# A decoder layer on one core: the last tiles of cross attention reordered, and four running sums instead of six in the shared expert

## What is computed

```python
x = x + attn(layernorm(x), Wqkv, bqkv, Wo, bo)
x = x + xattn(layernorm(x), ctx, mask, Wq, ..., residual_scale)
x = x + ffn(layernorm(x), gate, Wg, Wu, Wd, Sg, Su, Sd)
# ffn:
scores = softmax(x @ gate.T)                       # 64 experts
topk_w, topk_i = top_k(scores within the best 3 of 8 groups, 6)
pos = rank of the token among those that chose the expert
out = (silu(buf @ Wg.T) * (buf @ Wu.T)) @ Wd.T     # per expert, 192 slots
y = sum(out[slot] * topk_w, axis=1)
shared = silu(x @ Sg.T) * (x @ Su.T) @ Sd.T        # 704 inner features
return y + shared
```

## Time and profile before

| | |
|---|---|
| runs | 1564.96, 1571.54, 1579.25 us (median 1571.54) |
| profiled execution | 1564.96 us, span 1563.2 us |
| mean granted TensorE clock | 0.979 |
| TensorE busy | 1481.2 us (95%) |
| VectorE busy | 1135.9 us (73%) |
| ScalarE busy | 957.2 us (61%) |
| GpSimd busy | 713.1 us (46%) |
| steps 12 to 15 of cross attention | 540.15 to 607.67 us |
| cross attention after its loop | 607.67 to 654.25 us |
| routed experts | from 656.6 us to about 1377 us |
| end of the feed-forward | about 1377 to 1563.2 us |

### The profile page before, as it was taken

The page is one execution under the profiler, slowest core; times in us unless marked ns, Lnnn a source line. Parts: engine busy times, 40 slices in busy tenths (PEclk is TensorE's granted clock), DMA queues, the critical chain, the costliest instruction groups (busy, mean ns, idle before and its releaser), DMA issues.

```text
span 1563.2 us, 30303 instructions
## 1 busy us (share of the span) xinstructions
PE 1481.2 (95%) x10344; PEld 1224.2 (78%) x10344; DVE 1135.9 (73%) x2032; ACT 957.2 (61%) x1890; POOL 713.1 (46%) x885
## 2 busy tenths in 40 slices
PE   6999998999999988689999999999999999999988
PEld 4788886778888766478888888888888888866766
DVE  6677666646888789558777777777777877767766
ACT  4566566644566665558777877777777777741110
POOL 2122225333232143246556565665656555447763
PEclk9999999999999999889999999999999999999998
DMA  6012212332121221299877787777877778367664
GB/s 209 1 62 82 61 49 69 102 98 69 62 80 50 76 88 45 99 365 335 273 264 266 261 294 268 265 262 269 295 264 264 261 275 287 130 205 242 188 189 148
DMA packets 116629, 280.25 MB, mean 179 GB/s; under 512 B 17984, under 2 KB 23104, under 8 KB 116544
## 3 DMA queue, kind: packets, MB, share of 16 engines
q1 hardware_dynamic: 98800, 228.25, 42.9%
q0 software_dynamic: 15360, 50.34, 10.1%
q10 hardware_dynamic: 2384, 0.53, 0.2%
HBM read 235.69 MB, written 43.38 MB: 179 GB/s over the span
## 4 chain that ended last, share of the span: by engine, by line
PE 51%; DVE 2%; issue 1%; SPq 1%; DMA 1%; ACT 0%; POOL 0%; DVEq 0%; POOLq 0%
PE e_gu L2575 18%; PE e_gu L2577 8%; PE e_dn_rest L2603 5%; PE e_dn_main L41 3%; PE e_tr L49 3%; PE e_dn_main L43 3%; PE e_dn_main L42 3%; PE h_dn L41 1%; PE h_dn L42 1%; PE h_dn L43 1%; DMA e_raw_d<-in_L_ffn_Wd_dram 1%; SPq L2283 1%; PE h_gt L43 1%; PE h_gt L41 1%; PE h_gt L42 1%
## 5 line engine op out<-in xcount | busy, mean ns | idle before, releaser
L2338 POOL TENSOR_TENSOR e_hid<-e_h_raw,e_hid 128x128 fp32r<-128x128 f32 (+1 forms) x192 | 166.2, 866 | 222.6 <-ACT e_hid L2403 222.5
L2575 PE MATMUL e_gu<-e_xT_hi_lo,e_wg 128*128 128x384 f32 (+1 forms) x768 | 232.2, 358 | 0.8 <-issue 0.6
L2575 PE MATMUL e_gu<-e_xT_hi_lo,e_wu 128*128 128x384 f32 (+1 forms) x768 | 230.6, 356 | 0.0
L2577 PE MATMUL e_gu<-e_xT_hi_lo,e_wu 128*128 128x192 f32 (+1 forms) x768 | 193.4, 252 | 0.0
L2577 PE MATMUL e_gu<-e_xT_hi_lo,e_wg 128*128 128x192 f32 (+1 forms) x768 | 193.3, 252 | 0.0
L2346 POOL TENSOR_TENSOR e_wd<-e_raw_d,e_wd 96x512 fp32r<-96x512 f32 x64 | 131.8, 2059 | 35.9 <-ACT e_wd L2388 35.9
L2575 PEld LDWEIGHTS e_gu<-e_xT_hi_lo,e_wg 128*128 128x128 f32 (+1 forms) x768 | 138.4, 180 | 6.5 <-issue 1.8
L2481 DVE TENSOR_TENSOR e_total<-e_gu,e_low 128x384 f32<-128x384 f32 (+1 forms) x192 | 105.5, 550 | 51.8 <-issue 41.3
L2398 ACT ACTIVATE e_low<-e_gu 128x384 f32<-128x384 f32 (+1 forms) x192 | 93.4, 486 | 80.7 <-PE e_gu L2577 73.6
L2577 PEld LDWEIGHTS e_gu<-e_xT_hi_lo,e_wg 128*128 128x128 f32 (+1 forms) x768 | 140.1, 182 | 1.4
L2575 PEld LDWEIGHTS e_gu<-e_xT_hi_lo,e_wu 128*128 128x128 f32 (+1 forms) x768 | 137.9, 180 | 3.8
(11 more groups left out here) (419 smaller groups left out, 3957.6 us busy)
## 6 DMA issues: line engine op xcount, KB each, us to landing
e_raw_g<-in_L_ffn_Wg_dram SPq DMA_DIRECT2D x64, 704.0 KB
e_raw_u<-in_L_ffn_Wu_dram SPq DMA_DIRECT2D x64, 704.0 KB
e_raw_d<-in_L_ffn_Wd_dram SPq DMA_DIRECT2D x64, 512.0 KB, 6.4
y_dram<-e_y_main SPq DMA_DIRECT2D x64, 256.0 KB
e_raw_d<-in_L_ffn_Wd_dram SPq DMA_DIRECT2D x64, 192.0 KB, 7.5
y_dram<-e_y_rest SPq DMA_DIRECT2D x64, 128.0 KB
s_xr<-in_x_dram SPq DMA_DIRECT2D x16, 256.0 KB, 4.1
x_dram<-s_x SPq DMA_DIRECT2D x16, 256.0 KB, 2.4
```

What stands on the lines that cost most here:

```text
L2338: pool.tensor_tensor(hid[b][1][0:n, c, :], h_raw[g.odd][b][0:n, c, 0:P], hid[b][0][0:n, c, :].bitcast(F32), ALU.subtract).then_inc(s_hl, 1)
L2575: pe.matmul(bank[0:n, 0:2 * CAP], w[b][0][:, k, m:m + n], xT[:, :, k, toks], start=k == 0, stop=False)
L2577: ins = pe.matmul(bank[0:n, 0:CAP], w[b][1][:, k, m:m + n], xT[:, 0, k, toks], start=False, stop=k == KC - 1)
```

## The change

It has two parts. In `cross_phase`, for steps t >= 12 (`LAST`): TensorE's `turn_final(t-2)` moves behind `project_out(t-1)`, VectorE's `final_lo(t-2)` behind `output(t-1)`, and VectorE's `row_sums(t)` ahead of `choose_experts`. In steps 14 and 15 the second early unit moves behind `project_out`, on TensorE, and behind the table entries, on ScalarE. After the loop, `widen`, `project_out` and several units move ahead, so that the units fill other places between the steps of the routing, and ScalarE copies one more gate (`COPIED` = 4) and makes the entries of the last full group before units 8 to 10. In `shared_programs` the sums have four buffers instead of six, so the residual of tile n+4 is loaded when `finish(n)` is done, and VectorE's `routed` halves go to other places: one tile fewer is summed ahead of a turn and two to three halves more are done between the chunks of turns 1 and 2.

```diff
-AHEAD_SUMS = 6
-COPIED = 3
+COPIED = 4
...
+        LAST = BATCH - XQ
...   # ScalarE, in the loop: behind the table entries instead of ahead
+                for i in EARLY_UNITS.get(t, ())[1:2]:
+                    shared_out(i)
...   # ScalarE, after the loop
             rinv_out(BATCH - 1)
+            attn_hi(BATCH - 1)
             shared_out(4)
-            attn_hi(BATCH - 1)
             final_norm(BATCH - 2)
             final_hi(BATCH - 2)
             table_entries(NG - 3, 0)
+            shared_out(5)
+            table_entries(NG - 3, 1)
             route_exp(BATCH - 2)
             final_norm(BATCH - 1)
-            shared_out(5)
+            shared_out(6)
             final_hi(BATCH - 1)
-            table_entries(NG - 3, 1)
             route_exp(BATCH - 1)
             for c in range(COPIED):
                 shared_gate(c)
-            shared_out(6)
             shared_out(7)
-            table_entries(NG - 2, 0)
-            shared_out(8)
-            table_entries(NG - 2, 1)
-            shared_out(9)
-            shared_out(10)
+            for i in range(PAIR):
+                table_entries(NG - 2, i)
+            for i in range(8, INNER):
+                shared_out(i)
...   # VectorE, in the loop
-                if t >= 2:
+                if LAST > t >= 2:
                     final_lo(t - 2)
...
                     output(t - 1)
+                if t >= LAST:
+                    final_lo(t - 2)
...
                     route_max(t - 2)
+                if t >= LAST:
+                    row_sums(t)
                 for g in choosing:
                     choose_experts(g)
-                row_sums(t)
+                if t < LAST:
+                    row_sums(t)
...   # TensorE, in the loop
-                for i in EARLY_UNITS.get(t, ())[1:2]:
-                    shared_unit(i)
-                if t >= 2:
+                if LAST > t >= 2:
                     turn_final(t - 2)
...
                 project_out(t - 1)
+                for i in EARLY_UNITS.get(t, ())[1:2]:
+                    shared_unit(i)
+                if t >= LAST:
+                    turn_final(t - 2)
...   # TensorE, after the loop
+            widen(BATCH - 1)
             shared_unit(4)
-            widen(BATCH - 1)
             positions(BATCH, one)
             table_part(BATCH, one - 1)
+            project_out(BATCH - 1)
             turn_final(BATCH - 2)
-            project_out(BATCH - 1)
+            shared_unit(5)
             logits(BATCH - 2)
-            shared_unit(5)
+            shared_unit(6)
             turn_final(BATCH - 1)
             logits(BATCH - 1)
+            shared_unit(7)
             positions(BATCH, two)
-            shared_unit(6)
-            shared_unit(7)
+            shared_unit(8)
             table_part(BATCH, one)
-            shared_unit(8)
+            shared_unit(9)
             positions(BATCH, three)
-            shared_unit(9)
             shared_unit(10)
...   # shared expert: four sums
-            if n >= AHEAD_SUMS:
-                sp.wait_ge(s_o[n % 2], (n - AHEAD_SUMS) // 2 + 1)
+            if n >= 4:
+                sp.wait_ge(s_o[n % 2], (n - 4) // 2 + 1)
...   # shared expert: VectorE
-        late_half = range(TOPK // 2, TOPK)
-        chunks(0, {2: (0, 0), 3: (0, 1), 4: (1, 0)})
-        routed(1, late_half)
+        chunks(0, {3: (0, 0), 4: (0, 1)})
+        routed(1)
         finish(0)
         routed(2)
         finish(1)
         routed(3)
         finish(2)
         finish(3)
-        routed(4)
-        chunks(1, {0: (5, 0), 1: (5, 1), 2: (6, 0), 3: (6, 1), 4: (7, 0)})
-        routed(7, late_half)
+        chunks(1, {1: (4, 0), 2: (4, 1), 3: (5, 0), 4: (5, 1), 5: (6, 0)})
+        routed(6, range(3, TOPK))
         finish(4)
-        routed(8)
+        routed(7)
         finish(5)
-        routed(9)
         finish(6)
         finish(7)
-        routed(10)
-        chunks(2, {1: (11, 0), 2: (11, 1), 3: (12, 0), 4: (12, 1)})
+        chunks(2, {0: (8, 0), 1: (8, 1), 2: (9, 0), 3: (9, 1), 4: (10, 0), 5: (10, 1)})
         for c in range(SCN):
             hidden_lo(3, c)
         finish(8)
+        routed(11)
+        finish(9)
+        finish(10)
+        routed(12)
+        finish(11)
         routed(13)
-        finish(9)
+        finish(12)
         routed(14)
-        finish(10)
-        finish(11)
+        finish(13)
         routed(15)
-        for n in range(12, BATCH):
-            finish(n)
+        finish(14)
+        finish(15)
```

More of the change, by code:

```diff
@@ L971, in cross_uses @@
             ex[0] += [("xf", t - 2), ("lg", t - 2)]
-        proj += [("f", i) for i in EARLY_UNITS.get(t, ())]
+        early = EARLY_UNITS.get(t, ())
+        proj += [("f", i) for i in early[0:1]]
         if t <= BATCH:
             proj += [("o", t - 1)]
+        proj += [("f", i) for i in early[1:2]]
         proj += units[2:3]
@@ L1554, in _ @@
                     final_hi(t - 2)
-                for i in EARLY_UNITS.get(t, ())[1:2]:
-                    shared_out(i)
                 for m in cross_context(t):
@@ L2677, in shared_programs @@
         xT = [two(sb, "xT0_", [P, KC, QT * P], F32R)]
-        acc = [sb(f"acc{b}", [P, H]) for b in range(3)]
+        unused(4 * (4 * KC * M - 2 * KC * QT * P))
         act_g = two(sb, "act_g", [P, QT * P])
         h_raw = two(sb, "h_raw", [P, QT * P])
-        acc += [sb(f"acc{b}", [P, H]) for b in range(3, AHEAD_SUMS)]
+        acc = [sb(f"acc{b}", [P, H]) for b in range(4)]
         o_sb = two(sb, "o", [P, H])
-        unused(4 * (4 * KC * M - 9 * H) - 4)
+        unused(4 * (4 * KC * M - 10 * H) - 4)
         unused(4)
@@ L2702, in shared_programs @@
         s_dn = sem("down_in_psum")
-        s_x3 = [sem(f"x3_loaded{b}") for b in range(AHEAD_SUMS)]
+        s_x3 = [sem(f"x3_loaded{b}") for b in range(4)]
         s_rh = sem("raw_hidden_loaded")
@@ L2742, in load_x3 @@
         def load_x3(n):
-            a = n % AHEAD_SUMS
-            if n >= AHEAD_SUMS:
-                sp.wait_ge(s_o[n % 2], (n - AHEAD_SUMS) // 2 + 1)
-            sp.dma_start(acc[a][:], x3[tile(n) * P:(tile(n) + 1) * P, :]).then_inc(s_x3[a], 16)
+            if n >= 4:
+                sp.wait_ge(s_o[n % 2], (n - 4) // 2 + 1)
+            sp.dma_start(acc[n % 4][:], x3[tile(n) * P:(tile(n) + 1) * P, :]).then_inc(s_x3[n % 4], 16)
         def store(n):
@@ L2753, in sync @@
         sp.wait_ge(*free["gate_up_of_last"])
-        for n in range(AHEAD_SUMS):
+        for n in range(4):
             load_x3(n)
@@ L2768, in sync @@
                 store(n)
-                if n + AHEAD_SUMS < BATCH:
-                    load_x3(n + AHEAD_SUMS)
+                if n + 4 < BATCH:
+                    load_x3(n + 4)
         for b in range(2):
@@ L2860, in routed @@
             b = n % 2
-            to = acc[n % AHEAD_SUMS]
+            to = acc[n % 4]
             if ks[0] == 0:
-                dve.wait_ge(s_x3[n % AHEAD_SUMS], 16 * (n // AHEAD_SUMS + 1))
+                dve.wait_ge(s_x3[n % 4], 16 * (n // 4 + 1))
                 dve.tensor_copy(w_t[b][:], weight[:, tile(n) * TOPK:(tile(n) + 1) * TOPK]).then_inc(s_wt[b], 1)
@@ L2876, in finish @@
                 dve.wait_ge(s_st[b], 16 * (n // 2))
-            dve.tensor_tensor(o_sb[b][:], dn[b][:], acc[n % AHEAD_SUMS][:], ALU.add).then_inc(s_o[b], 1)
+            dve.tensor_tensor(o_sb[b][:], dn[b][:], acc[n % 4][:], ALU.add).then_inc(s_o[b], 1)
         def hidden_lo(p, c):
```

## The result

The changed kernel takes 1587.89 us in the median of 8 runs (1583.06 to 1592.85); the kernel before, in 8 runs on the same chip, 1572.98 us (1564.96 to 1579.25). The profiled execution took 1587.95 us, with a span of 1586.2 us against 1563.2, a difference of 23.0 us. That pair exaggerates: the profiled execution of the kernel before is its fastest.

What follows compares the result with a forecast made beforehand. TensorE was busy 1481.2 of 1563.2 us, with VectorE setting the pace in steps 13 to 15. Cross attention +7.3 and last stage -1.5 gave +5.8 us on the 1571.54 us median: 1577 us, range 1562 to 1590.

Steps and rivals of the forecast that it cites:

- the ring: Cross attention, steps 12 to 15: logits wait for transposes and `final_lo`, sums for logits, VectorE's next step for `row_sums`; +10.3 us.
- the clock's rival: Last stage and projections of steps 14 and 15: stalls lower the clock, rows land late; +14.7 us, 1586 us, chance 0.12.
- -3.0 behind the loop: Cross attention behind the loop: wait for table entries goes, last store is issued sooner; -3.0 us, bounds -4 and 0.
- -1.5 in the last stage: Shared expert: TensorE stalls go, new ones come, the end hangs on GpSimd's gathers; -1.5 us, bounds -4 and +6.
- sums and reciprocal: Each of steps 12 to 15, behind the logits: table sums and reciprocal take 2.02 us.
- `place_tokens(two)` ends at about the same place (+0.5 us): Behind the loop: placing the last full group ends only 0.5 us later, its entries 4.2 us sooner.
- the two stalls ahead of chunk 2: Last stage, turns 1 and 2: TensorE's stalls of 3.02 and 1.95 us go, with gains of 3.0, 2.4 and 2.0 us.
- `finish(1)` costs about 0.6 in turn 0: Last stage, turn 0: `finish(1)` stands behind one more half of `routed(1)`, costing about 0.6 us.
- The hidden ring: Rival, steps 12 to 15: VectorE's own work covers the logits, so no loss there; 1564.5 us, chance 0.17.
- Nothing that can be seen: Rival, whole kernel: the ring and tail cancel, within 3 us of 1571.5 us; chance 0.16.
- The gathers held up in full: Rival, last stage: VectorE's sums hold up three gathers, 10.8 us each instead of 8.6; +12.4 us, 1584 us, chance 0.05.

Runs made afterwards that it cites:

- loop_only: Kernel before with only the order of steps 12 to 15 changed; ratio 1.0099, +15.5 us, these steps 85.17 us against 67.52.
- tail_only: Kernel before with only the order behind the cross-attention loop changed, including the fourth copied gate; ratio 1.0000, 47.36 us behind the loop against 46.58.
- final_lo_late: Kernel before with one move, VectorE's `final_lo` behind `output` in steps 12 to 15; ratio 1.0073, +11 us, these steps 79.58 us.
- cross_only: Kernel before with the whole cross attention of the changed kernel, shared expert as before; ratio 1.0091, +14.3 us, median 1568.16 us.
- shared_eight_ahead: Kernel before with the changed shared expert, but `routed(8)` ahead of turn 2 and `routed(9)`, `routed(10)` at its first four chunks; ratio 1.0017.
- mended_again: Kernel before with the changed order behind the loop, positions ahead of unit 7, four sum buffers and other `routed` places; ratio 0.9958, 6.6 us faster.
- shared_only: Kernel before with only the shared expert changed, cross attention as before; ratio 1.0049, +7.7 us.
- after: The changed kernel with the whole diff, against the kernel before; median 1587.89 us, ratio 1.0091.

## Why the prediction was right, and where its size was wrong

The sign was right for the reason given, the ring. That the value fell inside the range is in part luck: the range (1562 to 1590) was wide, for the clock's rival and for the scatter of the runs, and 1587.89 us is at its upper end. Of the three terms of the sum two came out with the other sign: -3.0 behind the loop (+1.7 measured) and -1.5 in the last stage (+3.4 in the profiles, +7.7 for the shared expert alone).

**The ring** was right in place and sign: VectorE waits before `route_max` and the reciprocal in all four steps and before `final_lo` in steps 14 and 15, the steps got longer, and the loop is the whole loss of cross attention (loop_only against tail_only). It was mis-sized: +10.3 us forecast, +15.9 in the profile. By step +2.0, +3.2, +1.9, +3.2 against +4.4, +2.6, +3.3, +5.6. The failed term is the part behind the projection, the logits (1.43) and "sums and reciprocal" (2.02), which I priced at full clock from the earlier trace rows: of the 5.6 us that were missing 4.1 lie from the transposes to the end of the reciprocal. From the start of the transposes to the end of the reciprocal step 12 took 562.01 + 0.96 - 554.92 = 8.05 us, where the forecast had 3.9 + 2.0 (the logits 2.5 us for 1.43, sums and reciprocal 3.0 for 2.02), though TensorE reached the projection 7.4 us into the step (550.20 - 542.84), as it had reached the transposes before (547.52 - 540.15), and took 4.7 us for it against my 4.4. In steps 13 to 15 the same part took 6.4, 5.6 and 6.6 us for 5.9, 5.4 and 5.4. The rest lies ahead of the transposes: in steps 14 and 15 they start 13.7 us into the step (596.52 and 615.76) for my 12.5, behind table sums and first matmuls of the projection at the lower clock in step 14, and in step 15 because the slow matmuls of the step ahead also made the scores late, the 1.39 us wait at 605.85. Step 13 had it the other way: the projection took 2.9 us for my 4.2, at full clock from 569.68 on, behind a wait of 3.44 us. I had written a rival for the clock, but put it behind the stalls of the last stage and the projections; the short waits that my own change of order made, in front of the logits, had no clock cost in the sum.

**Which move does it.** The prediction tied the ring to the transposes behind the projection. final_lo_late shows that `final_lo` behind `output` is enough for most of it (+12.1 of 15.9 us), with the transposes and `row_sums` in their old places.

**Behind the loop** I said -3.0; it was +1.7, and +0.8 alone. The step that failed is "`place_tokens(two)` ends at about the same place (+0.5 us)". Before, the positions stood right behind the logits; the change puts unit 7 between them, at low clock:

```profile
651.34 0.77 PE L41 MATMUL c_sc<-a_shared_x_hi,a_shared_up_lo 128*128 128x512 f32 x1
...
656.71 0.30 PE L2031 MATMUL c_sc<-c_diag_pos,c_chosen 128*64 128x128 bf16 x2
```

```profile
657.33 0.42 DVE L1763 TENSOR_REDUCE c_lmax<-c_sc 64x2 f32<-64x256 f32 x1 [4.67 <-PE c_sc L2036]
```

The first fence is TensorE, the second VectorE. 5.4 us for that unit, and the placing starts 31.1 us into the stage instead of 25.7 (633.41 - 607.67). The gain that I had counted behind it (no wait of 2.66 us for the entries) came, with 0.85 us of the wait left, but on a stage that was already 5.3 us late. The bounds (-4 to 0) left the cost out.

**The last stage.** Right: the two stalls ahead of chunk 2 are gone, and the new ones stand before the last two of the 17 matmuls of the first down tile of turns 1 and 2, 2.20 and 2.00 us for my 2.4; gathers 13 to 15 come back to back and take 8.7, 9.5 and 8.2 us for my 8.6; the last `finish` hangs on `routed(15)`. TensorE:

```profile
1445.24 0.79 PE L41 MATMUL h_dn<-h_sd,h_hid 128*128 128x512 f32 x1 [2.55 <-DVE h_o L2884]
...
1490.62 0.50 PE L2990 MATMUL h_dn<-h_sd,h_hid_lo_over_hi 128*128 128x512 f32 x1 [2.20 <-DVE h_hid_lo_over_hi L2894]
...
1541.18 0.80 PE L2990 MATMUL h_dn<-h_sd,h_hid_lo_over_hi 128*128 128x512 f32 x1 [2.00 <-DVE h_hid_lo_over_hi L2894]
```

Wrong: the first of these rows. "`finish(1)` costs about 0.6 in turn 0" took the late half of `routed(1)` alone. But with `routed(0)` one chunk later gather 2 starts 5.6 us later (GpSimd, against 28.9 us behind the last `e_dn_rest`, now 34.5):

```profile
1430.46 0.19 POOL L2789 COPY h_idx<-slot 128x6 uint32<-128x6 uint32 x1 [13.63 <-DVE h_acc L2875]
```

`routed(2)` waits for its rows, `finish(1)` behind it, and TensorE for that: 2.55 us, and eight matmuls at the lower clock behind it. Turn 2 begins 108.8 us behind the last `e_dn_rest` (1504.75), against 108.6 before, not 3.8 us sooner; `routed(10)` so ends 4.0 us later than forecast, gather 13 starts 3.6 us later, and the last `finish` ends 4.8 us later. The moved sum was followed on VectorE but not through GpSimd's two buffers to the next gather but one. The diff also moves more than its description says: turn 1 has five halves of `routed` between its chunks as before and turn 2 six instead of four, and ahead of turn 2 three tiles fewer are summed (up to tile 7 instead of tile 10).

**The rivals.** The hidden ring is excluded: VectorE's waits in steps 12 to 15 sum to about 21 us, where it had less than 3. "Nothing that can be seen" is excluded by the ratio's interval. "The clock takes more" gave 1586 us, nearer to 1587.89 than the forecast. Its mechanism holds, but only in part at the places that it named: the 2.00 us stall of turn 2 was followed by the lower clock (0.80 us), the 2.20 us one of turn 1 was not (0.50 us); the projection of step 14 began at the lower clock (12 matmuls in 3.64 us), that of step 15 did not (2.87 us). So its number is near, though its parts did not come as it had them. The gathers held up in full are excluded: 8.2 to 9.5 us each, not 10.8. GpSimd while VectorE is in the six sums of `routed(12)` (1554.54 to 1559.23), and one transfer before them:

```profile
1553.57 0.95 POOL L2792 DMA_INDIRECT h_yk<-y_dram,h_idx  x1 [0.30 <-issue]
1554.82 1.29 POOL L2792 DMA_INDIRECT h_yk<-y_dram,h_idx  x1 [0.30 <-issue]
1556.42 1.27 POOL L2792 DMA_INDIRECT h_yk<-y_dram,h_idx  x1 [0.31 <-issue]
1557.99 1.27 POOL L2792 DMA_INDIRECT h_yk<-y_dram,h_idx  x1 [0.30 <-issue]
```

0.3 us for each transfer that meets the sums, 0.9 us in this gather; in the next one five transfers meet sums and it takes 9.5 us. By the rule that the prediction took from the Trainium skill (SBUF — State Buffer, "SBUF: two separate sides"), which the page limits, for two SBUF inputs, to a GpSimd operation that reads SBUF, the trace agrees in direction; no run here shows which part of a transfer is held up, and the size is that of these rows.

## What to carry to other kernels

An operation of 0.7 us can cost 11 us if it is moved past one that waits for the engine it feeds: ask of each moved instruction not how long it takes but what the next engine does between its old place and its new one. Price a new wait of TensorE of about 2 us once for itself, and give the case that the matmuls behind it run at the lower clock a chance of its own: in step 12 that cost as much again (8.05 us for 5.9), in step 13 next to nothing. Where a unit of independent matmuls can be put into the wait, put it there (3.9 to 4.9 us in two steps, by the profiles). And where a moved sum frees a gather buffer, follow it to the gather after the next before calling it free.

## What the runs showed of the hardware

Whether the clock falls depends here on when a wait comes, not only on how long it is. In self attention, some 50 us before its end and in code that all kernels share, TensorE transposes four times with waits for ScalarE between, the last of 1.47 us; cross_only and the kernel before:

```profile
245.69 1.11 PE L832 MATMUL s_sc<-ident,s_prb 128*128 128x128 f32 x4 [1.47 <-ACT s_prb L505]
```

```profile
245.34 0.66 PE L832 MATMUL s_sc<-ident,s_prb 128*128 128x128 f32 x4 [1.48 <-ACT s_prb L505]
```

In the 14 profiles this row starts between 245.16 and 246.56 us. In the seven where it starts at 245.56 or sooner it takes 0.65 or 0.66 us, and the granted clock from 245 to 250 us is 1.00; in the seven from 245.69 on it takes 0.70 to 1.11, the granted clock of that stretch is 0.50 to 0.70, and step 12 starts at 542.13 to 546.64 instead of 539.91 to 540.34. The changed kernel is among the late ones (246.56; its execution was already behind when SyncE issued the first `s_xr` loads, at 27.49 us against 26.24): the 2.7 us that it has lost by step 12 stand in code that the change leaves alone, and shared_eight_ahead and mended_again, which have the loop of the kernel before, have lost 2.7 and 2.0 us there. In the same way the 2.20 us stall before the last two matmuls of turn 1's first down tile is followed by a matmul of 0.80 us in shared_only and of 0.50 us in after. And in the changed kernel the matmuls behind waits of 1.96 us (step 12) and 2.55 us (last stage) ran at the lower clock, those behind 3.44 and 2.23 us (step 13) did not. I don't know how to forecast this; between tail_only (245.56) and cross_only (245.69) a shift of 0.13 us goes with 3.6 us at the start of step 12, so the length of a stage with short stalls in it, the last one here, has to be compared over several profiles.
